# Projection against a doubled diagonal matrix, and experts with the second matrix standing in the array

## The reference, cut to what matters

```python
# conv block: full + x_prune is the array y of the kernel (50176 x 64)
out = (full + x_prune) @ W_proj + b_proj
x   = x + out                                  # the array out, and x2 of the kernel
# experts
t      = layer_norm(x)                         # 50176 x 64
logits = t @ gate_w + gate_b                   # 8 columns
probs  = softmax(logits); idx = argmax(probs); prb = probs[idx]
pos    = number of earlier tokens with the same idx
kept   = pos < C                               # C = 7840 seats for each expert
buf[idx, pos] = t                              # the array xbuf of the kernel
hmid   = relu(buf @ w1 + b1)                   # 8 x 7840 x 256
ybuf   = hmid @ w2 + b2                        # 8 x 7840 x 64
x      = x + nan_to_num(ybuf[idx, pos] * (prb * kept))
```

## Time and profile before

| what | value |
|---|---|
| median of three executions | 10807.53 us |
| profiled execution, and its span | 10785.67 us, 10783.9 us |
| busy share of the span: PE, DVE, ACT, POOL | 74%, 80%, 70%, 22% |
| granted clock of PE over the span, share of full speed | 0.645 |
| project: first scatter to last, start us | 9325.8 to 9934.5 |
| experts: first and last instruction of PE, start us | 9964.1 and 10745.1 |
| experts: first and last store of POOL, start us | 9982.8 and 10774.9 |

### The profile page before, as it was taken

One profiled execution on the slowest core, in us unless ns is written; L12 is line 12 of the kernel. 1 busy time (PEld: TensorE's weight loads), 2 busy tenths in 40 slices (PEclk: granted clock), 3 DMA queues, 4 the chain that ended last, 5 costly groups with the idle time before them and its releaser, 6 DMA issues. The chain is left out here.

```text
span 10783.9 us, 168092 instructions
## 1 busy us (share of the span) xinstructions
PE 8031.3 (74%) x45265; PEld 5243.9 (49%) x45265; DVE 8632.9 (80%) x26258; ACT 7589.9 (70%) x12361; POOL 2352.2 (22%) x1944
## 2 busy tenths in 40 slices
PE   6776688867767777777787877885867678542998
PEld 6666455544434444444444444443434344442887
DVE  7888466659999999999999999998988999553443
ACT  5767122239979999999999999997979799321222
POOL 4666121210000000000000000000000000476767
PEclk9999865655656666666666666666656666555555
DMA  3332011100000000000000000000000000343111
GB/s 106 89 89 84 21 24 25 27 24 14 19 12 19 14 18 19 16 18 18 16 19 18 15 18 19 15 17 12 18 14 16 15 16 15 79 105 75 51 56 43
DMA packets 669928, 352.48 MB, mean 33 GB/s; under 512 B 587281, under 2 KB 605680, under 8 KB 665056
## 3 DMA queue, kind: packets, MB, share of 16 engines
q1 hardware_dynamic: 607920, 242.84, 10.5%
q0 software_dynamic: 58624, 60.72, 2.1%
q10 hardware_dynamic: 2384, 37.11, 0.9%
HBM read 200.20 MB, written 147.72 MB: 32 GB/s over the span
## 5 line engine op out<-in xcount | busy, mean ns | idle before, releaser
L1185 PE MATMUL a_psT<-a_qt,a_kt 74*122 74x366 bf16 x3456 | 1566.8, 453 | 807.3 <-ACT a_pT L1266 607.0
L1350 DVE MAX8 a_near<-a_below 122x8 f32<-122x219 f32 (+1 forms) x5760 | 1768.3, 373 | 0.1
L1188 PEld LDWEIGHTS a_psT<-a_weigh,a_drops 122*122 122x122 bf16 x10368 | 1585.2, 192 | 195.5
L1266 ACT ACTIVATE a_pT<-a_psT 122x732 f32<-122x732 f32 (+1 forms) x1920 | 1369.2, 713 | 433.4 <-PE a_psT L1188 428.7
L1343 DVE SCALAR_TENSOR_TENSOR a_below<-a_s,a_te,a_signs 122x1097 f32<-122x1097 f32 x1152 | 1547.5, 1353 | 140.7 <-remote 139.9
L1274 ACT ACTIVATE a_junk<-a_s,a_aim 122x1097 bf16<-122x1097 f32 x1152 | 1376.9, 1203 | 284.2 <-DVE a_s L1417 284.2
L1188 PE MATMUL a_psT<-a_weigh,a_drops 122*122 122x122 bf16 x10368 | 1534.7, 275 | 0.0
L1201 PE MATMUL a_psO<-a_pT,a_v 122*32 122x366 f32 x6912 | 1412.6, 703 | 0.0
L1274 ACT ACTIVATE a_signs<-a_s,a_te 122x1097 bf16<-122x1097 f32 x1152 | 1400.0, 1218 | 4.9 <-DVE a_te L1335 4.9
L1274 ACT ACTIVATE a_junk<-a_s,a_te 122x1097 bf16<-122x1097 f32 x1152 | 1387.3, 1207 | 0.0
L1515 POOL DMA_DIRECT2D a_dst<-o x15 | 13.8, 918 | 6184.4 <-DMA o<-a_o 6184.4
(11 more groups left out here) (375 smaller groups left out, 14377.0 us busy)
## 6 DMA issues: line engine op xcount, KB each, us to landing
xbuf<-r_blank ACTq DMA_DIRECT2D x16, 1990.6 KB
e_xg<-xbuf SPq DMA_DIRECT2D x56, 568.8 KB
r_bc<-pr SPq DMA_DIRECT2D x16, 1372.0 KB, 7.1
a_k<-kT SPq DMA_DIRECT2D x384, 51.5 KB
a_q<-qT SPq DMA_DIRECT2D x384, 51.5 KB
a_kt<-kT SPq DMA_DIRECT2D x384, 51.5 KB
a_qt<-qT SPq DMA_DIRECT2D x384, 51.5 KB
r_xt<-in_x SPq DMA_DIRECT2D x16, 784.0 KB
```

What stands on the lines that cost most here:

```text
L1185: pe.matmul(out[:, x, 0:CW], kt[q][:, u * QP:(u + 1) * QP], qt[q][:, c * CW:(c + 1) * CW], start=True, stop=False)
L1188: mm = pe.matmul(out[:, x, t * QP:(t + 1) * QP], drops[:, c * CT + t, u * QP:(u + 1) * QP], weigh[:, :], start=False, stop=t == CT - 1)
L1266: act.activation(pT[j % RING][:, 0:w, :], psT[(q + j) % 2][:, 0:w, 0:CW], ACT.Exp).then_inc(exped, 1)
L1350: mx = dve.max(near[:, t, g, :], below[t % 3][:, EDGES[g]:EDGES[g + 1]])
```

## The change

In project, `wproj` and `wgate` become 128 rows by 128 and by 16 columns, with the matrix twice on the diagonal and zeros elsewhere. DVE blanks both, and SP's loads of them wait for that (`emptied`). One product then makes two tiles: 14 products for a picture in place of 28, each 128 rows deep and 128 (or 16) columns wide. The tiles come out in order, eight to a PSUM bank, and `projected` is released bank by bank, so that DVE adds behind each bank. The logits lie in one bank, and one operation adds their bias.

In experts, three things change. (1) DVE copies the 64 channels of a chunk into a dense tile `e_xs` (`pack`), and `turn` becomes a transpose of two tiles at once, which waits for `packed` in place of the load. `e_psX` is now one bank in place of two. (2) In `outputs` w2 stands in the array, 64 columns of it for each of two tiles beside each other, and 224 (or 112) tokens stream by; the result comes out turned, 64 channels on partitions, ScalarE copies it out with the bias b2 (`bring`), and PE turns it back (`back`), two tiles in a transpose. The bank `e_psY` is a single one, and `e_psV` is double. (3) DVE multiplies each unit out of `e_psV` with the probability (three operations for a chunk) in place of two bias operations and one product. The bias b2 is loaded with channels on partitions, 512 single numbers for each of two halves, in place of a broadcast of 224 KB.

The diff, cut to what the prediction speaks of (the hunk in rank only orders names of semaphores, and `take`, `rectify` and the six last operations of DVE stay):

```diff
@@ -1542,7 +1542,7 @@
-        wproj, wgate = sb("p_wproj", [2 * C, C]), sb("p_wgate", [2 * C, E])
+        wproj, wgate = sb("p_wproj", [2 * C, 2 * C]), sb("p_wgate", [2 * C, 2 * E])
...
+        emptied = sem("p_emptied")
...
-        HERE = NT // 4
-        COUNTS_AT = 128
+        BANK = 8
+        BANKS = [(j, min(j + BANK, NT)) for j in range(0, NT, BANK)]
+        COUNTS_AT = 256
...
+            sp.wait_ge(emptied, 2)
             for h in range(2):
-                sp.dma_start(wproj[h * C:(h + 1) * C, :], d.wproj).then_inc(loaded, 16)
-                sp.dma_start(wgate[h * C:(h + 1) * C, :], d.wgate).then_inc(loaded, 16)
+                sp.dma_start(wproj[h * C:(h + 1) * C, h * C:(h + 1) * C], d.wproj).then_inc(loaded, 16)
+                sp.dma_start(wgate[h * C:(h + 1) * C, h * E:(h + 1) * E], d.wgate).then_inc(loaded, 16)
...
-                for r in range(NT // 2):
-                    for h in range(2):
-                        mm = pe.matmul(psP[:, 2 * h + r // HERE, r % HERE * C:(r % HERE + 1) * C],
-                                       yT[h * C:(h + 1) * C, r * TP:(r + 1) * TP], wproj[h * C:(h + 1) * C, :],
-                                       start=True, stop=True)
-                mm.then_inc(projected, 1)
+                for g, (j0, j1) in enumerate(BANKS):
+                    for j in range(j0, j1, 2):
+                        mm = pe.matmul(psP[:, g, (j - j0) * C:(j - j0 + 2) * C], yT[:, j // 2 * TP:(j // 2 + 1) * TP],
+                                       wproj[:, :], start=True, stop=True)
+                    mm.then_inc(projected, 1)
...
                 for r in range(NT // 2):
-                    for h in range(2):
-                        mm = pe.matmul(psL[h][:, r * E:(r + 1) * E], tT[h * C:(h + 1) * C, r * TP:(r + 1) * TP],
-                                       wgate[h * C:(h + 1) * C, :], start=True, stop=True)
+                    mm = pe.matmul(psL[0][:, 2 * r * E:2 * (r + 1) * E], tT[:, r * TP:(r + 1) * TP], wgate[:, :],
+                                   start=True, stop=True)
                 mm.then_inc(logits, 1)
...
-                dve.wait_ge(projected, b + 1)
-                for h in range(2):
-                    for g in range(2):
-                        mine = slice(2 * HERE * g + h, 2 * HERE * (g + 1) + h - 1, 2)
-                        dve.tensor_tensor(w[:, mine, C:2 * C], psP[:, 2 * h + g, 0:HERE * C].rearrange("p (j c) -> p j c", c=C),
-                                          xt[:, mine, :], ALU.add).then_inc(x2_made, 1)
+                for g, (j0, j1) in enumerate(BANKS):
+                    dve.wait_ge(projected, len(BANKS) * b + g + 1)
+                    dve.tensor_tensor(w[:, j0:j1, C:2 * C], psP[:, g, 0:(j1 - j0) * C].rearrange("p (j c) -> p j c", c=C),
+                                      xt[:, j0:j1, :], ALU.add).then_inc(x2_made, 1)
...
+            dve.memset(wproj[:, :], 0.0).then_inc(emptied, 1)
+            dve.memset(wgate[:, :], 0.0).then_inc(emptied, 1)
             dve.wait_ge(loaded, 16 * 6)
...
-        b2 = sb("e_b2", [TP, E, C])
+        b2 = sb("e_b2", [2 * C, E])
...
+        yT = [sb(f"e_yT{u}", [2 * C, HALF_WIDE]) for u in range(2)]
+        xs = [sb(f"e_xs{u}", [TP, XG, C]) for u in range(2)]
+        psX, psY = (ps(x, [2 * C, 512]) for x in ("e_psX", "e_psY"))
         psH = [ps(f"e_psH{u}", [128, 2, 512]) for u in range(2)]
-        psY = [ps(f"e_psY{i}", [TP, 512]) for i in range(2)]
...
+                sp.dma_start(b2[h * C:(h + 1) * C, :], d.b2.rearrange("e c -> c e"), allow_slow_non_contiguous=True).then_inc(loaded, 16)
...
-            sp.dma_start(b2[:, :, :].rearrange("p e n -> p (e n)"),
-                         d.b2.rearrange("(a e) n -> a (e n)", a=1).partition_broadcast(TP)).then_inc(loaded, 16)
...
-                    pe.wait_ge(x_in[c % 3], 16 * (c // 3 + 1))
-                if m >= 2:
-                    pe.wait_ge(x_out, m - 1)
+                    pe.wait_ge(packed, c + 1)
+                if m >= 1:
+                    pe.wait_ge(x_out, m)
                 for r in range(pairs):
-                    for h in range(2):
-                        mm = pe.matmul(psX[m % 2][h * C:(h + 1) * C, r * TP:(r + 1) * TP], xg[c % 3][:, first + 2 * r + h, 0:C],
-                                       k.ident[0:TP, 0:TP], start=True, stop=True)
+                    mm = pe.transpose(psX[:, r * TP:(r + 1) * TP],
+                                      xs[c % 2][:, first + 2 * r:first + 2 * r + 2, :].rearrange("p j c -> p (j c)"),
+                                      k.ident[0:TP, 0:TP])
                 mm.then_inc(turned, 1)
 
...
             def outputs(m):
                 c, first, pairs = place(m)
-                e = c // XC
+                e, n = c // XC, pairs * TP
                 pe.wait_ge(relud, 2 * (m + 1))
-                for g in range(2 * pairs):
-                    half, at = divmod(XG * c + first + g, XU)
-                    r, h = divmod(g, 2)
-                    if at == 0 and half >= 2:
-                        pe.wait_ge(y_taken, half - 1)
-                    for i in range(2):
-                        mm = pe.matmul(psY[half % 2][:, at * C:(at + 1) * C], hT[m % 2][:, i, h, r * TP:(r + 1) * TP],
-                                       w2[:, e, i, :], start=i == 0, stop=i == 1)
+                if m >= 1:
+                    pe.wait_ge(y_out, m)
+                for i in range(2):
+                    for h in range(2):
+                        mm = pe.matmul(psY[h * C:(h + 1) * C, 0:n], w2[:, e, i, :], hT[m % 2][:, i, h, 0:n],
+                                       start=i == 0, stop=i == 1)
                 mm.then_inc(outed, 1)
 
-            pe.wait_ge(loaded, 16 * 5)
-            for m in range(-2, UNITS):
+            def back(m):
+                c, first, pairs = place(m)
+                pe.wait_ge(y_out, m + 1)
+                if m >= 2:
+                    pe.wait_ge(v_made, m - 1)
+                for r in range(pairs):
+                    mm = pe.transpose(psV[m % 2][:, r * 2 * C:(r + 1) * 2 * C], yT[m % 2][:, r * TP:(r + 1) * TP], k.ident[:, :])
+                mm.then_inc(backed, 1)
+
+            pe.wait_ge(loaded, 16 * 6)
+            for m in range(-2, UNITS + 1):
                 if m + 2 < UNITS:
                     turn(m + 2)
                 if 0 <= m + 1 < UNITS:
                     hidden(m + 1)
-                if m >= 0:
+                if 0 <= m < UNITS:
                     outputs(m)
+                if m >= 1:
+                    back(m - 1)
...
 
-            act.wait_ge(loaded, 16 * 5)
-            take(0)
-            for m in range(UNITS):
-                if m + 1 < UNITS:
-                    take(m + 1)
-                rectify(m)
+            def bring(m):
+                c, first, pairs = place(m)
+                e, n = c // XC, pairs * TP
+                act.wait_ge(outed, m + 1)
+                if m >= 2:
+                    act.wait_ge(backed, m - 1)
+                act.activation(yT[m % 2][:, 0:n], psY[:, 0:n], ACT.Identity, bias=b2[:, e:e + 1]).then_inc(y_out, 1)
+
+            act.wait_ge(loaded, 16 * 6)
+            for m in range(-2, UNITS):
+                if m + 2 < UNITS:
+                    take(m + 2)
+                if 0 <= m + 1 < UNITS:
+                    rectify(m + 1)
+                if m >= 0:
+                    bring(m)
 
         @block.vector
         def _(dve):
             link = Chain(dve, k.chain)
-            dve.wait_ge(loaded, 16 * 5)
-            flat = "p j c -> p (j c)"
+
+            def pack(c):
+                dve.wait_ge(x_in[c % 3], 16 * (c // 3 + 1))
+                if c >= 2:
+                    dve.wait_ge(turned, PER_CHUNK * (c - 1))
+                dve.tensor_copy(xs[c % 2][:, :, :], xg[c % 3][:, :, 0:C]).then_inc(packed, 1)
+
+            pack(0)
             for c in range(CHUNKS_ALL):
-                e, x, y = c // XC, xg[c % 3], yo[c % 2]
-                bias = b2[:, e, :].unsqueeze(1).to_broadcast([TP, XU, C])
-                for g in range(2):
-                    dve.wait_ge(outed, PER_CHUNK * c + PER_CHUNK - 1 + g)
-                    dve.tensor_tensor(v[:, g * XU:(g + 1) * XU, :],
-                                      psY[g][:, 0:XU * C].rearrange("p (j c) -> p j c", c=C), bias,
-                                      ALU.add).then_inc(y_taken, 1)
+                x, y = xg[c % 3], yo[c % 2]
+                if c + 1 < CHUNKS_ALL:
+                    pack(c + 1)
+                for u, (first, pairs) in enumerate(XUNITS):
+                    m = PER_CHUNK * c + u
+                    dve.wait_ge(backed, m + 1)
+                    tiles = slice(first, first + 2 * pairs)
+                    dve.tensor_tensor(v[:, tiles, :], psV[m % 2][:, 0:2 * pairs * C].rearrange("p (j c) -> p j c", c=C),
+                                      x[:, tiles, 2 * C + 1].unsqueeze(2).to_broadcast([TP, 2 * pairs, C]),
+                                      ALU.mult).then_inc(v_made, 1)
```

(5 more changed lines are left out.)

32 lines of the change are left out of this document (15 added, 17 removed).

## The result

Six runs of the changed kernel have a median of 10757.99 us (10731.63 to 10765.13), six of the kernel before beside them 10802.83 us (10779.51 to 10817.57). The ratio is 0.9952, 95% interval 0.9932 to 0.9972: 0.5% faster, 45 us. The forecast was 10786, with a range from 10762 to 10960; it fell short of the gain. Measured again later, beside three variants, the change has 10736.74 us (10731.39 to 10751.12) against 10798.42 for the kernel before, ratio 0.9940 (0.9917 to 0.9962): 62 us.

A forecast was written before the change was run, and what follows sets the result against it. POOL was taken to bound project, PE experts with POOL 0.5 us behind. PE's start at 9967, 56 chunks of 13.8 us and the tail gave 10761, 23 under the earlier span, so median 10786 us; range 10762 to 10960.

The forecast's parts named there:

- against the profiled execution: Whole kernel: summed to 10761 us, 23 us under the earlier profiled span, then carried to a median of 10786 us.
- 28 us in all: Experts: POOL is 0.5 us a chunk behind PE, so it keeps whatever PE gains beyond that.
- start: Start of experts: changed b2 loads +1.5 us (bounds -2 and +4), first copy 0.6; PE starts at 9967.
- loop: Experts: 56 chunks of 13.8 us, less the last stall of 5.1, plus 1.5 to fill, ending at 10736.
- tail: End of experts: DVE's tail 4.9 us, nine POOL steps 11.3, the last step and all behind it 9.0.
- Project beside POOL: Project: runs at POOL's scatter pace, hiding PE and DVE changes; only the first scatter moves, +1 us (0 to +3).
- The price of outputs: Experts: new outputs cost the same as hidden, 1.79 us for four tiles and 1.13 for two, at the low clock.
- The new wait: Experts: at every chunk PE stands through DVE's tail until the copy lands, 5.1 us (4.8 to 5.6).
- The clock: Experts: clock falls in each stall and rises 4 us after restart; PE's work 8.6 us a chunk (8.3 to 10.0).
- Rival A: Experts: clock stays low for most of each chunk; period 16.9 us, 10960 us in all; chance 0.23.
- Rival C: Experts: POOL alone is the bound, period 13.46 us; 10764 us in all, faster by 0.4%; chance 0.14.
- POOL "with hardly a wait": Experts: a sign that POOL's steps should stay at 1.25 us with hardly a wait.

The follow-up runs named there:

- the two later groups: Later run sets: the change's experts with project as in the kernel before, 10739.02 us; and the unmodified change measured again, 10736.74 us.
- the old list with a stall: Kernel before, with PE's turning of a chunk's last unit made to wait until DVE finished the previous chunk: 11115.31 us, ratio 1.0300.
- the old turning with new outputs: The change with chunks turned by the old products straight from the loaded chunk, without copy; new outputs and turning back kept: 10731.94 us, ratio 0.9935.
- The version with the early copy and half the stores: The change with DVE's copy of chunk c+2 issued before chunk c's last unit, and every second experts store left out: 10463.34 us, ratio 0.9692.
- the half stores: The change with every second store of experts left out, output incomplete: 10719.32 us, ratio 0.9922 to the kernel before.
- the second group: Runs on one chip sharing the kernel before, 10798.42 us, with variants that add copies, a stall or the old turning, and the change again, 10736.74 us.
- the longer wait: The change with DVE's copy of 640 elements made three times at each chunk instead of once: 10796.11 us, ratio 0.9991 to the kernel before.

## Why the prediction was wrong, and where it was right

**The base.** The step that failed is the sum "against the profiled execution", carried over to the median as it stood: "23 us under the span of before", so 22 under the median. It holds only if that execution's stage is a usual one. It was not: 837.3 us against 869.6, 869.8 and 875.6. The prediction saw the three stretches in part (it took the high level of the earlier trace rows from one, and the fall of the clock of the earlier trace rows at another's end) but used the mean of 13.95 us over the 56 chunks as the kernel's pace, and not as one draw; by the same sum the others have 14.7 to 14.8. So the cap on what PE can gain before POOL holds it, "28 us in all", came to 70 us or more. The error was hidden in part because the same execution came late to experts (project ended at 9946.2, mean 9934.1): 12 of the 33 us did not show in the whole, and the other 21 are the 0.2% by which it lay under the median, which the prediction saw and carried along as if they were outside experts. With the usual numbers before is 9934 + 870 = 10804, as measured; and after is 9934 + 804 = 10738, near the 10739 and 10737 of the two later groups, but 20 us under the 10758 of the result, and this rest is open. The change in experts is then -66 us: 23 that the forecast had, 33 that its base lacked, and 10 by which its stage of 814 us was too long. From the usual base that stage gives 10748, below the range's lower end.

**The sum of the stage.** Forecast, without project's +1: start 19.6, loop 769.2, tail 25.2, together 814.0. Measured in the profile after: PE's first instruction 14.8 us after the stage's start, 757.5 to PE's last, and 34.0 from there to the span's end, 806.3. Three terms were mis-sized. The start by -4.8: each of the two loads of b2 (L1856) took 0.63 or 0.64 us of SP's queue, as short as that of b1 (L1857), and the load of w2 stood 3.95 where it had stood 5.59:

```profile
9938.46 0.63 SPq L1856 DMA_DIRECT2D e_b<-in_L_ffn_b  x1
...
9940.49 0.62 SPq L1857 DMA_DIRECT2D e_b<-in_L_ffn_b  x1
9941.15 3.95 SPq L1858 DMA_DIRECT2D e_w<-in_L_ffn_w  x1
9945.15 2.19 SPq L1851 DMA_DIRECT2D e_xg<-xbuf  x3
```

The loop by -11.7: 0.13 us a period over 55 is 7; the fill and the last chunk (5.84 us between DVE's last operations) must be the rest. The tail by +8.8: the forecast let PE's last chunk come without a stall and POOL still be idle for it; but then POOL is a chunk behind, and 20 stores follow PE's last instruction, not 10.

**Point by point.**
- Project beside POOL: right. Stage 689 in both, POOL's scatters 1060 ns for 1057, DVE's wait for them 106 us for 95. The new projection of one picture took 6.20 us at the low level, forecast 6.3 at most. The first scatter came 67.3 us into the stage in place of 68.7, earlier by 1.4 where +1 was forecast; over all profiles it is 67.1 to 69.6 us with the new project and 68.6 to 70.4 with the old.
- The price of outputs, as `hidden`: right. 1.76 us for 1.79 at the low level; one after the other they would have cost 3.2 by the prediction's sum, so the two tiles in columns ran beside each other. The Trainium skill has this rearrangement in "TensorEngine Tiling (Array Packing)", When to Use Tiling: with a streamed dimension of 64, swap what stands and what streams and pack columns. The trace agrees: by these rows the old 3.25 us became 1.76, with 0.47 more for the turning back.
- The new wait: right in place and size. 54 stalls on the copy behind the start of the stage, 4.82 us in the chunk shown and 4.7 in the mean, forecast 5.1. Its two terms without a row, 0.4 us until DVE wakes and 0.1 until PE does, are 0.36 (10103.89 to 10104.25) and 0.05 in the chunk shown. Lengthening the stall by 1.0 to 1.2 us lengthened the mean period by 0.8, so its length counts nearly whole.
- The clock: right in kind, and 1 us late. It rises 5.1 us after the restart, not 4, and PE's work is 13.67 - 4.82 = 8.85 us, not 8.6. The two misses in work and stall cancel, and that the period came out at 13.67 for 13.7 is in part luck. The reason given (the old outputs keep the clock low, the new list does not) was an inference from 5 us at the start of experts; the old list with a stall, against the old turning with new outputs, bears it out. Its other support was read too strongly. The rise of the earlier trace rows stands behind 14 transposes, but these stand behind 5.49 us of products without a gap:

```profile
9271.29 5.49 PE L1634 MATMUL p_psP<-p_wproj,p_yT 64*112 64x64 f32 x56 [0.51 <-ACT p_yT L1672]
9276.71 3.02 PE L1622 MATMUL p_psT<-ident,p_y 112*128 112x112 f32 x14
```

So it shows no rise from transposes alone, and "after 3.3 us" counts only the last part of the work. Nor are a third of the new list's instructions transposes: they are 10 of 58 a chunk. No run here has transposes alone.

- Rival A, that the clock stays low, held 0.23 on the strength of 370 us of dense work at the low level. That row spoke of the old list alone. The version with the early copy and half the stores runs the new list at 0.89. Rival C named the right end (10764) for a wrong reason: POOL alone does not hold the change at 13.46, PE's loop holds it at 13.67, as the half stores show.
- POOL "with hardly a wait": right, 14 waits of 58 us in all, 45 of them the start. Its steps were 1.34 us in the mean (1042 ns and 0.30), not 1.25; the prediction's own 13.46 for ten said so.
- The case of tiles that do not overlap: the 16.1 us are nearer 15.8 by the rows; nothing hangs on it.
- A kernel faster by over 0.3% was given a chance of 0.20, and it came.

## What to carry to other kernels

Before a sum is hung on one profiled execution, ask which of its stretches would be otherwise in the next: here the granted clock was high in three stretches of a stage of identical chunks, and the usual stage was 33 us longer. A stage whose period has several values (15.2 us here, and 8.3 to 13.5 in and behind a stretch of high clock) has a base with a spread, and a change that makes the period uniform can take this spread away: the 23 runs of the kernel before in the second group lie 86 us apart, the 10 with the longer wait 34 and the 6 of the change 20 (fewer runs, which makes for a part of it). When the last turn of a loop loses its stall, look at the engine behind it: what the first one gains there the second may owe.

## What was not expected of the hardware

- The old list, busy without a gap for 459 us, kept the clock at 0.50, and with a stall of 5.34 us at every chunk it was high for only 34 of 1137 us. The new list's clock went up and down once in every chunk, 6.8 us at each level, 55 stretches in all (the first 10.2 us long), the same in three executions. A stall 1 us longer turned this even pace into a cycle of four chunks. With the stores halved and the copy early it was high for 388 us of the stage's 534.
- The high stretches of the old list were 37.5 us at the start and 30.7 us later, each time the same lengths, while whether and where they came differed between executions.
- The start of experts moved by up to 27 us between executions of the same code ahead of it.
